# Moving half a query projection, the context statistics and four weight splits within the last self-attention body

## What is computed

```
x   = x + gate_a * (softmax(q k^T) v @ W_proj + b_proj)      # self-attention
q_c = ln(x) @ W_qc + b_qc                                    # "c" below
k_c, v_c = split(ln(context) @ W_kvc + b_kvc)
x   = x + softmax(q_c k_c^T) v_c @ W_cproj + b_cproj         # cross-attention
x   = x + gate_m * mlp(modulate(ln(x)))
```

## Time and profile before

| | us |
|---|---|
| median of three runs | 2610.44 |
| the profiled execution | 2611.72 |
| its span | 2609.9 |
| PE busy in the span | 2571.6 (99%) |

### The profile page before, as it was taken

One profiled execution on the slowest core, in us unless ns is written; L12 is line 12 of the kernel. 1 busy time (PEld: TensorE's weight loads), 2 busy tenths in 40 slices (PEclk: granted clock), 3 DMA queues, 4 the chain that ended last, 5 costly groups with the idle time before them and its releaser, 6 DMA issues.

```text
span 2609.9 us, 50236 instructions
## 1 busy us (share of the span) xinstructions
PE 2571.6 (99%) x18696; PEld 2127.4 (82%) x18696; DVE 1695.0 (65%) x3399; ACT 1127.6 (43%) x2192; POOL 1274.4 (49%) x1426
## 2 busy tenths in 40 slices
PE   8999999999899999999999999999899999999999
PEld 6688888888788888888888888887678888888887
DVE  6677777777767777777777777776764444444442
ACT  4354454444535555555555555554542222212111
POOL 1445454454536777777777777775421121220230
PEclk9999999999999999999999999999899999999999
DMA  7554545555554444444444444433521111111110
GB/s 224 133 134 125 136 120 131 129 125 133 146 147 114 122 107 118 112 111 117 112 117 108 123 117 109 122 95 101 150 93 45 37 45 34 44 49 37 45 53 17
DMA packets 193045, 269.89 MB, mean 103 GB/s; under 512 B 34788, under 2 KB 112612, under 8 KB 192788
## 3 DMA queue, kind: packets, MB, share of 16 engines
q1 hardware_dynamic: 187116, 254.16, 36.9%
q0 software_dynamic: 3264, 7.92, 0.9%
q10 hardware_dynamic: 2424, 4.61, 0.7%
HBM read 111.11 MB, written 36.77 MB: 57 GB/s over the span
## 4 chain that ended last, share of the span: by engine, by line
PE 69%; DVE 1%; issue 0%; DMA 0%; ACT 0%; SPq 0%; DVEq 0%; ACTq 0%
PE late_sc_ps L1782 7%; PE late_or_ps L1811 5%; PE late_even_ps L72 5%; PE late_sc_ps L72 5%; PE late_even_ps L73 5%; PE late_even_ps L74 5%; PE late_sc_ps L74 5%; PE late_sc_ps L73 5%; PE shared_tr_ps L1798 4%; PE late_odd_ps L72 3%; PE late_odd_ps L74 3%; PE late_odd_ps L73 3%; PE late_tr_ps L1798 3%; PE late_odd_ps L1743 1%; PE late_tr_ps L72 1%; PE late_tr_ps L74 1%
## 5 line engine op out<-in xcount | busy, mean ns | idle before, releaser
L1970 DVE TENSOR_REDUCE cross_parts<-late_sc_ps 112x1 f32<-112x500 f32 x512 | 335.5, 663 | 219.3 <-PE late_sc_ps L1782 218.3
L2224 POOL TENSOR_TENSOR cross_part<-cross_prT 125x448 f32<-125x448 f32 x232 | 271.6, 1171 | 214.6 <-ACT cross_prT L2148 177.2
L1294 POOL TENSOR_TENSOR self_psum<-self_prT 112x224 f32<-112x224 f32 x256 | 178.3, 697 | 327.4 <-ACT self_prT L1160 318.3
L2626 ACT ACTIVATE mlp_hv<-late_sc_ps,mlp_b 128x512 f32<-128x512 f32 x112 | 77.2, 689 | 511.3 <-PE late_sc_ps L74 496.9
L2148 ACT ACTIVATE cross_prT<-shared_tr_ps 125x448 f32<-125x448 f32 x379 | 206.5, 545 | 164.3 <-PE shared_tr_ps L1798 158.3
L2226 POOL TENSOR_TENSOR cross_part<-cross_part,cross_prT 125x448 f32<-125x448 f32 x232 | 268.1, 1156 | 18.2
L1782 PE MATMUL late_sc_ps<-cross_kst,cross_qst 96*112 96x500 f32 (+1 forms) x1024 | 261.2, 336 | 3.5 <-DVE cross_parts L1970 1.7
L2148 ACT ACTIVATE cross_prT<-late_tr_ps 125x448 f32<-125x448 f32 x380 | 206.8, 544 | 109.4 <-PE late_tr_ps L1798 106.6
L2540 DVE CAST mlp_hT_h<-mlp_hv 128x512 fp32r<-128x512 f32 x112 | 57.0, 509 | 300.1 <-ACT mlp_hv L2626 300.1
L1160 ACT ACTIVATE self_prT<-self_st_ps 112x448 f32<-112x448 f32 x256 | 138.6, 542 | 167.3 <-PE self_st_ps L629 165.7
L1782 PEld LDWEIGHTS late_sc_ps<-cross_kst,cross_qst 96*112 96x112 f32 x1024 | 164.3, 178 | 18.3 <-DVE cross_parts L1970 2.6
(11 more groups left out here) (402 smaller groups left out, 7280.0 us busy)
## 6 DMA issues: line engine op xcount, KB each, us to landing
cross_kst<-cross_nat_h SPq DMA_DIRECT2D x508, 93.8 KB, 2.2
cross_kst<-cross_nat_l SPq DMA_DIRECT2D x254, 93.8 KB, 2.2
cross_qst<-qc SPq DMA_DIRECT2D x192, 112.0 KB, 2.4
cross_c_in<-in_context SPq DMA_DIRECT2D x78, 224.0 KB
self_kst<-self_nat_h SPq DMA_DIRECT2D x128, 112.0 KB, 2.3
self_qst<-self_natq_h SPq DMA_DIRECT2D x128, 112.0 KB, 3.0
self_x_in<-in_x SPq DMA_DIRECT2D x16, 448.0 KB, 3.8
self_kst<-self_nat_l SPq DMA_DIRECT2D x64, 112.0 KB, 2.2
```

What stands on the lines that cost most here:

```text
L1294: pool.tensor_tensor(psum[:, j], prT[:, j, 0], prT[:, j, 1], ALU.add).then_inc(p_summed, 1)
L1970: dve.tensor_reduce(parts[:, g % 2, j, u, 0:1], sc_ps[u][0:QN, 0:SHALF[0]], AX_X, ALU.max, negate=True).then_inc(maxed, 1)
L2224: pool.tensor_tensor(part[:], prT[:, j, 0:2], prT[:, j, 2:4], ALU.add).then_inc(pre_summed, 1)
```

## The change

Three tables, the order of SP's queue and the place of `low_context` in DVE's steps change. No operation is added or dropped.

- c(1, 0, 12) goes from step 15 of body 14 to step 4 of body 15, ahead of the first "ty"; c(1, 1, 12) goes from step 3 to step 5, ahead of the second.
- Context statistics: three tiles in step 4 and three in step 5 become one in step 5 and five in step 6. The inverse deviation goes from step 6 to 7, the mean term from 7 to 8, the normalization from steps 7 to 11 to steps 9 to 12.
- Low parts of W_kvc, pieces 4 to 7: from steps 14, 15, 16, 17 to 17, 18, 19, 20, and the high parts with them, each one step ahead.
- `low_context` stands before the statistics of y and before `low_wkv`.
- SP: the store of c of sequence 12 goes behind the first four loads of W_kvc.

```diff
-                       [("c", 0, 0, B - 4)], [("c", 0, 1, B - 4)], [("c", 1, 0, B - 4)]],
-               B - 1: [[("v", 0, 0, B - 1)], [("v", 0, 1, B - 1)], [], [("c", 1, 1, B - 4)],
-                       [("ty", 0, 0, B - 3)], [("ty", 1, 0, B - 3)], [], [("c", 0, 0, B - 3)],
+                       [("c", 0, 0, B - 4)], [("c", 0, 1, B - 4)], []],
+               B - 1: [[("v", 0, 0, B - 1)], [("v", 0, 1, B - 1)], [], [],
+                       [("c", 1, 0, B - 4), ("ty", 0, 0, B - 3)], [("c", 1, 1, B - 4), ("ty", 1, 0, B - 3)], [], [("c", 0, 0, B - 3)],
...
-        STATS_AT = ({4: (0, 1, 2), 5: (3, 4, 5)}, {NH + 3: range(ST)})
-        INVERSE_AT, MEAN_AT = (6, NH + 5), (7, NH + 7)
-        NORMAL_AT = ({7: (0,), 8: (1,), 9: (2,), 10: (3,), 11: (4, 5)}, {NH + 11: (0, 1, 2), NH + 12: (3, 4, 5)})
+        STATS_AT = ({5: (0,), 6: (1, 2, 3, 4, 5)}, {NH + 3: range(ST)})
+        INVERSE_AT, MEAN_AT = (7, NH + 5), (8, NH + 7)
+        NORMAL_AT = ({9: (0,), 10: (1,), 11: (2, 3), 12: (4, 5)}, {NH + 11: (0, 1, 2), NH + 12: (3, 4, 5)})
         TILES_AT = {12: (0,), 13: (1,), 14: (2, 3), 15: (4, 5)}
-        WKV_AT = (9, 10, 11, 12, 14, 15, NH, NH + 1)
+        WKV_AT = (9, 10, 11, 12, NH + 1, NH + 2, NH + 3, NH + 4)
...
-                if b.c == B - 1:
-                    store_qc(y3)
                 if b.c == B - 1:
                     sp.wait_ge(v_ps, 2 * B)
                     load_wkv(range(KC))
+                if b.c == B - 1:
+                    store_qc(y3)
...
+                    for t in TILES_AT.get(seam_step(b, h), ()):
+                        low_context(0, t)
                     if prv and h == (12 if b.c == B else 15):
                         stats(z, y, summed, lambda t: z.n(2, t + 1), st2, mv2, stats2, mvs2)
...
                         low_wkv(WKV_AT.index(seam_step(b, h)))
-                    for t in TILES_AT.get(seam_step(b, h), ()):
-                        low_context(0, t)
```

## The result

The changed kernel takes 2615.01 us, median of 21 runs (2610.08 to 2620.85), against 2610.88 for the kernel before (21 runs, 2606.29 to 2616.41): a ratio of 1.0016, with a 95% interval of 1.0010 to 1.0022, or +2.6 to +5.7 us. That is inside the forecast's range, and the ratio is within 0.2% (the interval's upper end is just above it), but the forecast was +1.6 and the measurement says +4.1: a small loss, clear of zero.

The account below looks back on a forecast made before the run. PE, busy 99%, bounds the program, with DVE nearly full in body 15. Terms -0.3 (body 15) and +1.9 (wait at `cross_k(0)`) sum to +1.6 us, forecast 2612.0 us, range 2608 to 2615.8.

Parts of the forecast that it names:

- part 7: W_kvc's last low part stands behind `low_y` in step 20: PE waits 1.9 us before `cross_k(0)`, at most 2.7.
- part 1: c(1, 0, 12) leaves step 15 of body 14: PE then awaits the last row maximum, 0.27 of 1.33 us won.
- part 6: Body 15, W_kvc loads, store, POOL and low parts: cost nothing; the 1.54 us wait at 701.56 stays.
- parts 2, 3 and 5: Body 15: removed half becomes a wait; halves return, second "ty" 1.3 us later; DVE holds p(0, 0), gain 0.3 us.
- part 2: c(1, 1, 12) leaves step 3, body 15: half turns into a wait of about 2.1 us for an exponential.
- The DMA at step 6: Body 15: PE's wait for the DMA placing the maxima is covered; bounded by 0 and 0.6 us, taken as 0.
- part 4: Body 15, `pv` and sums from 679.69: if the clock stays up, PE is 1.3 us ahead at step 7.
- rival (C): New waits at 670.5 and before `cross_k(0)` halve the clock: one fall +5.0 us, two +8.4; chance 0.12.
- The signs of being wrong: p(0, 0) starting before 689.5, no wait before the first product for k, or half clock in body 16.
- A: DVE is not last before p(0, 0): PE keeps 1.3 us and 0.3 more, sum -0.1, 2610.3; chance 0.17.
- B: No wait at `cross_k(0)`, low part ready in time: -0.3 to -2.2 us, 2609.2 in the middle; chance 0.12.
- D: Falls of the clock go away later in the program: a gain of over 5.2 us; chance 0.04.

Follow-up runs that it names:

- part 7 alone: The kernel before with only W_kvc's pieces 4 to 7 moved to steps 17 to 20: 2614.21 us against 2611.61, ratio 1.0010.
- the filled wait: The changed kernel with 20 transposes of the identity on PE ahead of the wait before the first product for k: 2612.93 us, ratio 1.0007.

## Why the prediction was right, and where it was not

**Right: within 0.2%, on the slower side, because of part 7.** The wait at the first product for k was forecast at 1.9 us and took 1.82, three times (the changed kernel twice, part 7 alone once). Its way is the one told: ACT's copy, `low_y` 0.62, low part 0.68. The longer bound of 2.7 wasn't reached. By the page "GPSIMD Engine Reference" of the Trainium skill, section Specifications, contention was possible; the last low part took 0.68 us here, with POOL's sum beside its last 0.2 us, so this case's trace doesn't bear it out for that piece. Another piece, at 700.45, took 1.46 in the changed kernel as one had before. The prediction took that for a single case, but it is the rule for this piece: 1.43 to 1.46 us in all twelve profiles that split it in step 11, each time beside POOL's product for y (L1302).

**Right: part 1** (0.26 us won, 0.27 forecast), **part 6** (PE's wait for y is 1.55 us, 1.54 before) **and most of the form of parts 2, 3 and 5**: the waits for the exponential, for `low_y` and, small (0.3 us), for the eviction ahead of p(0, 0) are there. The one for `normalize` ahead of `pv` is not, since the DMA wait stands in its place. ACT's wait for the mean term is gone, and p(0, 0) starts when DVE has evicted.

**Off: part 2's size, and with it the -0.3 of the sum.** I forecast that the removed half would turn whole into a wait of about 2.1 us. The wait was 0.84, so the scores of step 4 came 1.07 us earlier and not 0.27. The 0.8 us are one number: ACT's last two context DMAs, 1.64 us in the row that I took, take 0.82 to 1.02 in all ten other profiles that issue them as two pairs (in two of these the first pair was long instead, 1.98 and 2.29). Part 7 alone, whose body 15 is the old one, has 0.88 there, and its p(0, 0) at 37.38 shows that this didn't matter before. I priced a term by one row that was an outlier, and one which the old order hid. From there on the steps hold, 0.8 us early. DVE's `normalize` was forecast 1.39 us later than before (677.65 against 676.26) and came 0.61 later (23.76 against 23.15 us behind the first maxima). From its start to the eviction in front of p(0, 0) DVE took 690.97 - 679.29 = 11.68 us; forecast was 689.6 - 677.65 = 11.95, with 0.3 allowed for overlap. So 0.8 and 0.3 make up the 1.03 that p(0, 0) gained.

**Off: the DMA at step 6**, taken as covered, made PE wait for 0.89 us, outside my bound of 0 to 0.6. I had reasoned from the maxima being turned earlier; the row says that they don't land earlier for it. It cost little, since DVE set the end of this stretch.

**Off: part 4's fall.** It went from 6.83 us to 3.41, from 682.34 on; the window from 676.05 now has a clock of 0.96, where it had 0.51. The scores of step 7 came 1.31 us earlier (27.67 against 28.98 us behind the first maxima), as part 4 has it with the clock up, though only a part of that is the clock's. That the old fall cost nothing, being beside a full DVE, fits the stages, but no run tried it by itself.

**Off: the price of part 7.** The sum had the wait, 1.9, and not what follows it. I had the clock as a rival (C) with a chance of 0.12, of it 0.04 for one fall, and argued against it from the wait of 1.54 us at 701.56, behind which the clock stayed up. Behind the wait of 1.82 us it fell each time, in three profiles of three (and in none of the other ten at that place, the filled wait among them). The place was C's and the price was not: the fall lasts 3.41 us and not 6.83, and it costs 1.62 (41.50 less 39.88), not 3.4. The Trainium skill (TensorE: Matmul & The Clock Gate, A second HAM failure mode: psum-queue depth-cycling) speaks of repeated short gaps; here a single one, with PE full for 22 us before it, was followed by a fall.

**The sum**, with measured terms: -1.23 + 1.86 + 1.62 = +2.25 us on PE's way, where -0.3 + 1.9 = +1.6 stood. The two errors, 0.9 too little gain and 1.6 too little loss, cancel in part, and the forecast came out nearer than its terms. That is luck. The range held the first median, 0.8 us below its end, because it took in one fall of the clock. The medians moved by 4.1 and 2.6 us. The second agrees with 2.25; the first, with an interval from 2.6 up, is a little more. The fall behind the gap at cross-attention, 1.5 us in the profile of the first and absent in that of the second, would make up such a difference, but how often each kernel meets it isn't known. Of the 5.3 us between the profiles of the kernel before and the changed one 2.4 lie ahead of the change. Whether a systematic part of a microsecond is among them, these runs leave open.

**The signs of being wrong.** The prediction named three, and two of them occurred. In the time of the profile before, p(0, 0) starts at 653.11 + 36.30 = 689.41, ahead of 689.5, and the clock is at half in body 16. So by its own signs the forecast was wrong in its terms, though not in its range: part 2's wait and the price of part 7 are the steps that failed.

**The rivals.** A was right in its direction, not in its condition: PE kept 1.2 us, but DVE was still last before p(0, 0), with a wait of 0.3 us. Its size was wrong too: the 1.3 and 0.3 us that it names make 1.6 and not 2.0, so its time should have read 2610.7. B, no wait, was wrong; the two starts in the earlier trace rows decided it. C was the part that I undervalued. D did not occur.

## What to carry to other kernels

Before moving work later, ask whether it now stands behind something that hangs on PE's own latest output: such a wait can't be outrun, however early PE comes. In a stretch where PE is otherwise full, allow for a new wait of about 2 us its own length and about as much again for the clock behind it (it came in three of three profiles behind 1.82 us, in seven of 13 behind 1.62 us), and see whether one step less (here the low parts in steps 16 to 19) avoids the wait. And take a term's duration from more than one row where there are others; judge effects of 1 or 2 us by the length of a stage between two common instructions, not by totals that scatter by 5, and look behind the end of the stage for a fall of the clock that it leaves out.

## What the runs showed of the hardware that was not expected

- A single wait of 1.82 us in a full PE was followed in three of three profiles by 3.4 us at half the clock (0.52 to 0.53 in the windows shown, which begin a little ahead of it), beginning 0.2 to 1.1 us after the wait's end. With 20 transposes in 2.35 us in its place the clock stayed at 1.00. Of the twelve profiles with the wait of about 1.5 us for y, 25 us earlier, one had such a fall behind it: in the kernel that splits piece 7 one step earlier, where body 15 had run at half the clock before. Its PE timeline and its window:

```profile
705.60 0.62 PE L702 MATMUL shared_tr_ps<-shared_ident,cross_c_in 125*128 125x125 f32 x4 [1.54 <-DVE self_y L857]
```

```profile
706.90:710.30 3.40, 3.40 (x33) 2.33 (x26) 2.39 (x5) 0.96 (x2) 3.32 (x2) 0.52 0.23 67
```

- Behind the gap of 1.62 us ahead of cross-attention, the same in all 13 profiles, the clock fell for 3.41 us in seven and stayed up in six, at 1.5 us for a fall.
- The issue of the same two context DMAs held ACT for 0.82 to 1.64 us (and of the first two for 1.11 to 2.29), with the same program ahead of it at 1.64 (the kernel before) and 0.88 (part 7 alone).
- The small DMAs of the maxima seem tied to the context load: the scores behind them started 8.4 to 10.2 us after its first DMA, though their own issue lay between 0.7 and 3.6 us behind it, and the last packets of both ended within 0.6 us of each other.
- The same 650 us of program ahead of the change took 650.5 to 655.5 us from profile to profile, twice the effect that was to be measured.
